# Where the first context slice is loaded and rounded, and where GpSimd adds the last bias of tile 14, in a cross-attention kernel on one core

## The reference

```
# adapter with a router, over 8 experts; lora_A is 4 slices (64 wide) of the context, summed
logits = x @ router_W.T + router_b;  w = softmax(logits)
a_sum  = x @ lora_A summed over its four parts
x      = clip_nonfinite(x + 0.5 * sum_n w_n * (a_sum @ lora_B[n].T))
# cross attention with 32 heads of 32
Q = x @ Wq.T + bq;  K = ctx @ Wk.T + bk;  V = ctx @ Wv.T + bv
attn = softmax(where(mask, Q K^T / sqrt(32), -inf));  c = attn @ V
y = x + c @ Wo.T + bo
out = (y - mean(y)) / sqrt(var(y) + 1e-5) * ln_g + ln_b
```

## Time and profile before

| What | Value |
|---|---|
| Median of three executions | 643.59 us (643.53 to 644.02) |
| The profiled execution | 643.8 us, of which the span is 641.9 us |
| TensorE busy | 629.0 us, 98% of the span |
| VectorE busy | 500.7 us, 78% |
| ScalarE busy | 337.7 us, 53% |
| GpSimd busy | 268.0 us, 42% |
| Chain that ended last | 95% TensorE, 2% VectorE, 1% DMA, 1% issue |

### The profile page before, as it was taken

One profiled execution on the slowest core, in us unless ns is written; L12 is line 12 of the kernel. 1 busy time (PEld: TensorE's weight loads), 2 busy tenths in 40 slices (PEclk: granted clock), 3 DMA queues, 4 the chain that ended last, 5 costly groups with the idle time before them and its releaser, 6 DMA issues.

```text
span 641.9 us, 10730 instructions
## 1 busy us (share of the span) xinstructions
PE 629.0 (98%) x3455; PEld 544.9 (85%) x3455; DVE 500.7 (78%) x907; ACT 337.7 (53%) x1000; POOL 268.0 (42%) x357
## 2 busy tenths in 40 slices
PE   8999999999999999999999999999999999999993
PEld 8988889888988889888888888888888888888883
DVE  5689995578457774677468899999999999999635
ACT  6454463123242242322268778787777787777520
POOL 0020001000020002000335556888888998888874
PEclk9999999999999999999999999999999999999997
DMA  8936685436774467722857993425354344522312
GB/s 299 410 128 177 178 306 179 156 82 210 233 264 149 114 235 240 280 80 68 258 151 261 383 376 96 132 99 181 82 165 150 117 148 120 174 85 84 114 50 99
DMA packets 103399, 114.14 MB, mean 178 GB/s; under 512 B 57008, under 2 KB 76080, under 8 KB 103344
## 3 DMA queue, kind: packets, MB, share of 16 engines
q1 hardware_dynamic: 103152, 113.20, 53.4%
q10 hardware_dynamic: 192, 0.26, 0.2%
HBM read 67.29 MB, written 46.14 MB: 177 GB/s over the span
## 4 chain that ended last, share of the span: by engine, by line
PE 95%; DVE 2%; DMA 1%; issue 1%; ACT 0%; DVEq 0%; SPq 0%; POOL 0%; POOLq 0%; ACTq 0%
PE ps L602 26%; PE ps L603 26%; PE ps L604 26%; PE ps L664 4%; PE ps L747 4%; PE ps L760 2%; PE ps L761 2%; PE ps L635 1%; PE ps L638 1%; PE ps L636 1%; PE ps L674 1%; DMA stage<-WkT 1%; DVE u_lo L885 0%; DVE cx_sum L981 0%; DVEq L209 0%
## 5 line engine op out<-in xcount | busy, mean ns | idle before, releaser
L1258 POOL TENSOR_TENSOR u_sb<-a_sb,w_sb 128x512 f32<-128x512 f32 x16 | 19.6, 1245 | 236.2 <-DVE w_sb L879 231.3
L602 PE MATMUL ps<-wo_hi,cx_hi 128*128 128x512 f32 (+1 forms) x264 | 105.9, 401 | 0.0
L1185 ACT ACTIVATE s_sb<-s_sb,s_min 128x64 f32<-128x64 f32 x256 | 85.8, 338 | 34.6 <-DVE s_min L959 34.6
L604 PE MATMUL ps<-wo_hi,cx_lo 128*128 128x512 f32 (+1 forms) x264 | 101.7, 385 | 0.0
L603 PE MATMUL ps<-wo_lo,cx_hi 128*128 128x512 f32 (+1 forms) x264 | 101.6, 385 | 0.0
L602 PE MATMUL ps<-act_hi,w_hi 128*128 128x512 f32 x256 | 100.9, 394 | 0.3 <-DVE q_sb L933 0.3
L603 PE MATMUL ps<-act_lo,w_hi 128*128 128x512 f32 x256 | 99.8, 390 | 0.0
L604 PE MATMUL ps<-act_hi,w_lo 128*128 128x512 f32 x256 | 99.8, 390 | 0.0
L1150 ACT ACTIVATE act_hi<-h_t 128x512 fp32r<-128x512 f32 x32 | 20.3, 633 | 111.8 <-DVE h_t L922 111.8
L981 DVE SCALAR_TENSOR_TENSOR cx_sum<-ps,bias_c,cx_raw 64x256 f32<-64x256 f32 x128 | 61.8, 483 | 8.8 <-ACT cx_raw L1199 4.8
L1269 POOL TENSOR_TENSOR s_sb<-s_sb,s_inv 128x512 f32<-128x512 f32 x64 | 67.0, 1047 | 0.0
(11 more groups left out here) (119 smaller groups left out, 1543.1 us busy)
## 6 DMA issues: line engine op xcount, KB each, us to landing
q_cols<-q_sb SPq DMA_DIRECT2D x32, 512.0 KB, 3.6
qb<-q_cols SPq DMA_DIRECT2D x64, 256.0 KB, 4.0
x_sb<-xT SPq DMA_DIRECT2D x32, 256.0 KB, 3.2
h_rows<-hn_sb SPq DMA_DIRECT2D x64, 128.0 KB, 3.0
output_weights<-wo_sb SPq DMA_DIRECT2D x32, 256.0 KB, 2.5
z_sb<-h_rows SPq DMA_DIRECT2D x16, 512.0 KB, 4.7
out<-z_sb SPq DMA_DIRECT2D x15, 512.0 KB, 2.9
stage<-WvT SPq DMA_DIRECT2D x8, 512.0 KB, 4.6
```

Source lines behind the costliest of these rows:

```text
L602: pe.matmul(dst, lh, rh, start=(first and j == 0), stop=False)
L604: mm = pe.matmul(dst, ll, rh, start=False, stop=(last and j == n - 1))
L1185: act.activation(s_sb[c % 4][:, h, :], s_sb[c % 4][:, h, :], ACT.Exp, bias=s_min[c % 2][:, h:h + 1], scale=-1.0, accum_out=s_sum[c % 2][:, ...
```

## The change

Four edits. The DMA of context part 0 is issued by ScalarE, as its first instruction and ahead of the load of its function table, and no longer by SP as its second. The rounding of part 0 is done by VectorE (a copy into float32r) as its first instruction, no longer by ScalarE between two weight halves, and has a semaphore of its own, `first_hi`. The zeros for TensorE's first 7 matmuls are set by GpSimd as its first instruction of the program, on 128 x 128 elements in place of 128 x 512, and the matmuls read one column of them 512 times as the moving operand. On GpSimd the two `shift` halves of tile 14 stand ahead of `newton` of tile 15, in the same step.

```diff
@@ sync: loads @@
             load_half(0, 0)
-            load_context(0)
             load_half(0, 1)
@@ tensor @@
             for n in range(WARM):
-                pe.matmul(ps_up[0], act_hi[:, 0, 0:P], act_hi[:, 0, :], start=True, stop=True)
+                pe.matmul(ps_up[0], act_hi[:, 0, 0:P], act_hi[:, 0, 0:1].to_broadcast([P, TOK]), start=True, stop=True)
...
                 if k == 0:
-                    pe.wait_ge(ctxhi_done, 1)
+                    pe.wait_ge(first_hi, 1)
@@ vector @@
-            dve.memset(act_hi[:, 0, :].bitcast(F32), 0.0).then_inc(warm_set, 1)
+            first = CTX_PARTS[0]
+            dve.wait_ge(ctx_in[0], 16)
+            dve.tensor_copy(ctx_hi[:, first, :], ctx_t[:, first, :]).then_inc(first_hi, 1)
 
             def context_in(part):
                 ks = CTX_PARTS[part]
-                dve.wait_ge(ctxhi_done, part + 1)
+                if part == 0:
+                    dve.wait_ge(first_hi, 1)
+                else:
+                    dve.wait_ge(ctxhi_done, part)
@@ scalar @@
+            act.dma_start(ctx_t[:, CTX_PARTS[0], :], ctx_v[:, CTX_PARTS[0], :]).then_inc(ctx_in[0], 16)
             act.preload_act_table_set("natural_log_exp_and_others")
 
             def context_in(part):
+                if part == 0:
+                    return
@@ gpsimd @@
+            pool.memset(act_hi[:, 0, 0:P].bitcast(F32), 0.0).then_inc(warm_set, 1)
             pool.memset(ident[:], 0.0).then_inc(ident_set, 1)
...
                 for at_c, n in ((3, tile_at(s, 0, 2)), (7, tile_at(s, 1, 2))):
                     if c == at_c and live(n, TILES):
+                        if n == TILES - 1:
+                            for half in range(2):
+                                shift(n - 1, half)
                         newton(n)
...
-                    if c == at_c and live(n, TILES - 1):
+                    if c == at_c and live(n, TILES - 1) and (stage_, n) != (shift, TILES - 2):
                         stage_(n, half)
```

More of the change, by code:

```diff
@@ L323, in xattn_kernel @@
         stage_hi, stage_lo = sem("stage_hi"), sem("stage_lo")
-        ctxhi_done, ctxlo_done, a_step, mask_step = sem("ctxhi_done"), sem("ctxlo_done"), sem("a_step"), sem("mask_step")
+        first_hi, ctxhi_done, ctxlo_done, a_step, mask_step = sem("first_hi"), sem("ctxhi_done"), sem("ctxlo_done"), sem("a_step"), sem("mask_step")
         k_mm, k_bank, k_copied, v_mm = sem("k_mm"), sem("k_bank"), sem("k_copied"), sem("v_mm")
```

## The result

The changed kernel takes 640.38 us (median of six executions, 639.77 to 641.9), the kernel before 643.79 us (six, 643.53 to 644.55). The ratio is 0.9948 with a 95% interval of 0.9937 to 0.9958: 3.4 us faster, where 3.2 us were forecast. The profiled execution took 639.82 us, with a span of 638.0; it is one of the quicker ones. Its span is 3.9 us under that of before, half a microsecond more than the medians say.

The account below looks back on a forecast made before the run. TensorE, busy 98% of the span, bounds the middle; only start and end could gain. End 2.9 us (1.91 + 0.2 + 0.8) plus start 0.3 make 3.2, so 643.6 becomes 640.4 us, range 639.8 to 641.6.

Parts of the forecast that it names:

- The end: After GpSimd's tile 14 work moves earlier: VectorE, SP issue and last landing together save 2.9 us.
- VectorE 1.91: Last two VectorE operations (L1057): 1.42 us in place of 3.33, saving 1.91; bounds 0 and 1.95.
- Landing: Last store of tile 15: 2.1 us from issue to landing in place of 2.9, saving 0.8; bounds 0 and 0.9.
- SP's issue: Tile 15's second-half store: issued sooner after VectorE's end because tile 14 is stored earlier, saving 0.2 us; bounds 0 and 0.3.
- The cover of the moved pair: GpSimd before `newton` of tile 15: tile 14's `shift` halves fit in its idle wait, with 1.6 us of room.
- The start: First weight and context loads up to L664: saves 0.3 us, bounds -0.1 and 0.6.
- By the DMA: L635 at the start: SP's earlier issues bring it 0.4 us earlier, from 8.83; bounds 0 and 0.47.
- By TensorE: TensorE's own work in `keys(0)`: allows L635 at 8.40 + 0.15 - 0.1, giving 8.45; nothing taken for an earlier clock rise.
- the first half would land up to 0.3 us later: First weight half, sharing DMA with the context slice: up to 0.32 us later; 0.15 taken.
- x as the next bound: At L664: x's last piece lands near 20.25 us, so only 0.3 to 0.35 of the 0.38 us gain passes.
- Rival 3: At the start: TensorE's clock rises later because of new gaps, costing 1.1 us, time 641.5 to 641.8; chance 6%.
- Rival 1: The start gives nothing, as the context slice only moves to another issuer; 640.7 us; chance 20%.

Follow-up runs that it names:

- the end alone: The kernel before with only GpSimd's two additions of tile 14 moved ahead of `newton` of tile 15; 640.61 us, ratio 0.9941.
- the 8-column kernel: The changed kernel with GpSimd's tile 14 additions back behind `newton` of tile 15, each on 8 columns in place of 512; 641.33 us, ratio 0.9960.
- start alone: The changed kernel without the move of tile 14's `shift` halves on GpSimd, so only the edits at the start; 643.62 us, ratio 0.9986.
- the small load: The changed kernel with the 4 KB router bias loaded second on SP, where the context load stood before; 640.53 us, ratio 0.9936.
- the zeros at 1.43: The changed kernel with VectorE clearing 128x512 as before, so the zero matmuls start at 1.43 us; 640.33 us.
- the last group: Four kernels on one chip: changed again 639.96 us; with 8 zero matmuls 640.17; 8 plus `ctx_lo` ahead of `w_lo` 639.74; with 9 zero matmuls 639.82.

## Why the prediction was right

**The end** was forecast at 2.9 us and gave 3.17 in the profile and 3.4 in the medians of the end alone. Term by term: VectorE 1.91 forecast, 3.33 - 1.41 = 1.92 measured, and by the 8-column kernel it is GpSimd's long operation beside it that made the difference. Landing 0.8 forecast, 2.9 - 2.0 = 0.9 measured; the reasoning from 512 KB on idle queues less the time of 256 KB gave 1.95 and was the better number than the 2.1 chosen. The mechanism of the end is shown by the end alone and by the 8-column kernel. What is left for SP's issue is about 0.3, where 0.2 was put. The cover of the moved pair was there: GpSimd idled 1.63 us after it, 1.6 had been worked out.

**The start** was forecast at 0.3 us. The profiled pair shows 0.7, the medians 0.4 (start alone against before, not clear of zero). Each taken against the kernel before beside it, the changed kernel gained 3.4 and 4.2 us and the end alone 3.4, which leaves anything from nothing to 0.8 for the start. So 0.3 isn't refuted and isn't shown, and that the sum came within 0.2 us of the measured gain is partly luck.

The sum had L635 at the later of two times, 8.43 by the DMA and 8.45 by TensorE's own work. Both were too late for the profiled execution.
- By the DMA: "For L635 the bounds are 0 and 0.47" was mis-sized. The half of block 1 for which L635 waits was taken up by ScalarE at 6.34 in place of 7.32, 0.98 earlier, although its DMA was issued only 0.47 earlier, and a later place in SP's order put it back (7.18 with the small load). An issue moved up gained about twice its own length here. That it is because the engines' free time before 5 us was filled fits the bytes moved by then, but no run isolates it.
- By TensorE: the last matmul of `keys(0)` starts at 7.90 in place of 8.28, and this is what set L635, since no wait is left ahead of it. Nearly all of these 0.38 us come from the pace, which doubled near 5.2 and not at 6.5, and for which the sum had taken nothing. That is luck of the execution: with the same order of DMAs and the zeros at 1.43 the pace doubled at 7.2 and L635 came at 8.74, again with no wait, 0.09 us ahead of the kernel before. So of the 0.81 us by which L635 came earlier, 0.43 is the wait that the change removed and 0.38 is TensorE's.

That the first half would land up to 0.3 us later was right in sign: ScalarE starts on it at 3.79, not 3.58 (0.2; 0.15 taken). The rounding on VectorE took 0.29, against 0.24. The first real matmuls didn't come 0.3 us earlier, at 4.3, but at 4.56, held by ScalarE's rounding of that half, which had landed later; the sum took next to nothing from them.

**x as the next bound** was right: with `keys(1)` at 8.0 to 8.3 TensorE does wait for x, by 0.2 to 0.4 us in all four traces of the last group. It was put too late, though: the sum had x at 20.25, and in the profiled execution L664 started at 19.71.

**Rival 3 was under-rated.** Its price was 1.1 us and its chance 6 in 100. A late doubling is seen in two of the 14 profiles (9.4 and 10.2), and 4 of 10 times of the changed kernel and 6 of 12 of the start alone lie some 1.1 to 1.3 us above the others; how many of those were late doublings isn't known, since they weren't profiled but for one. It was written as a property of the kernel, either there or not; it is one of the single execution. The kernel before and the end alone spread as widely, so the times don't show that the change made it more frequent. The Trainium skill's "TensorE: Matmul & The Clock Gate", in "What's actually happening", has a gate whose periods don't start with the kernel. The traces agree: with the same 7 zero matmuls from 0.97 us on, the doubling came at 5.2, 5.6, 5.9, 6.9, 7.0 and 9.4 us.

**Rival 1** (no gain at the start) rests open within the noise of the times: no interval separates the start alone from zero. The traces speak against it, by the wait of 0.43 us that is gone. The Trainium skill's "DMA: Bandwidth & Descriptors", in "Issuing engines are not separate DMA queues", says that another issuer saves only its issue time. That isn't contradicted: with the small load in its place the slice's other issuer alone brought nothing. But what an issue's time is worth wasn't its length.

## What to carry to other kernels

At the end of a kernel look at what other engines still do for earlier tiles: an operation of GpSimd on SBUF beside a VectorE operation with two SBUF inputs cost VectorE 1.9 us here, and the store that waited for it cost another 1.2 us, about half in the issue and half in the landing of the last stores. If the engine idles before its last task, put the older work there. At the start, count the places in the first queue. Before a gain there is put down to an edit, look at when TensorE's pace doubled in each of the two executions, and judge by many executions and not by one profile; whether dummy work right up to the first real matmul helps, these runs leave open.

## What the runs showed of the hardware that was not expected

- The second half of block 0 was issued 0.47 us earlier and was there 1.2 us earlier: ScalarE took it at 5.76 before and by 4.5 after (its two operations at 3.79 run in a row for 1.37 us), and at 5.69 with a 4 KB load in between.
- The moment at which TensorE's pace doubles differed by over 4 us between executions with the same start (5.2 and 9.4), and the price at L664 was 1.6 us.
- A landing of 256 KB took 2.0 us from issue, with another 256 KB issued 0.7 us ahead, against 2.7 to 2.9 behind 512 KB more.
